# Long attention rows: a plain maximum for the unmasked half, taken as the initial value of the masked half's fused minimum

## The reference

```
att = q @ k.T * scale                      # (1024, 1024) for each of 2 x 16 heads
att = where(causal, att, -inf)
att = softmax(att, axis=-1)                # needs the maximum of each row's unmasked part
y   = att @ v
```

## Time and profile before

| what | value |
|---|---|
| median of three runs | 2633.96 us |
| lowest and highest run | 2629.57 and 2639.21 us |
| span of the profiled execution | 2632.3 us |
| TensorE, busy share of the span | 2535.4 us, 96% |
| VectorE | 1533.2 us, 58% |
| ScalarE, GpSimd | 1035.6 us (39%), 981.6 us (37%) |
| line 1501, 768 fused row pieces, busy | 413.2 us, mean 574 ns |

### The profile page before, as it was taken

How to read it: one execution, slowest core, us unless ns; L and a number is a source line. 1 busy time by engine, 2 the same in 40 slices (tenths; PEclk the granted TensorE clock), 3 DMA queues, 4 the chain that set the end, 5 groups by cost and what they waited for, 6 DMA issues and landing times.

```text
span 2632.3 us, 44135 instructions
## 1 busy us (share of the span) xinstructions
PE 2535.4 (96%) x16928; PEld 2013.0 (76%) x16928; DVE 1533.2 (58%) x3356; ACT 1035.6 (39%) x1885; POOL 981.6 (37%) x1373
## 2 busy tenths in 40 slices
PE   6999989999999999999999999999999999999999
PEld 4788867667668888888888878677776678888887
DVE  7777579979975445433333345798589643333333
ACT  6555346656653223311111133566466431111111
POOL 5333566666643225211111122666366521111110
PEclk9999989999999999999999999999999999999999
DMA  4222131222220110100000002343233100000001
GB/s 148 73 73 73 39 76 46 51 68 64 48 93 1 36 45 12 37 25 25 24 25 25 25 17 58 92 94 75 52 88 79 37 32 25 24 25 25 25 17 64
DMA packets 72002, 128.73 MB, mean 49 GB/s; under 512 B 15728, under 2 KB 24944, under 8 KB 71792
## 3 DMA queue, kind: packets, MB, share of 16 engines
q1 hardware_dynamic: 71792, 125.92, 17.3%
HBM read 62.42 MB, written 13.63 MB: 29 GB/s over the span
## 4 chain that ended last, share of the span: by engine, by line
PE 81%; DVE 6%; POOL 2%; ACT 2%; SPq 2%; issue 2%; DMA 1%; DVEq 0%; ACTq 0%; POOLq 0%
PE psum L1049 65%; PE psum L1167 5%; PE psum L1130 4%; PE psum L1148 4%; PE psum L1178 2%; DVE psum L1501 2%; SPq L1745 1%; PE psum L1058 1%; DVE s1a0rden L1540 1%; ACT s1a0e L1335 1%; SPq L1764 0%; POOL s1a0e L1671 0%; ACT s4a1e L1335 0%; PE psum L1137 0%; POOL rstd L1610 0%
## 5 line engine op out<-in xcount | busy, mean ns | idle before, releaser
L1501 DVE CUSTOM_DVE_ANT_0 psum<-psum,mask_q 128x512 f32<-128x512 f32 (+5 forms) x768 | 413.2, 574 | 101.2 <-PE psum L1130 97.3
L1049 PE MATMUL psum<-hA_hi,wmem 128*128 128x256 f32 (+1 forms) x1536 | 405.2, 334 | 0.5 <-DVE s1a0negmax L1501 0.3
L1049 PEld LDWEIGHTS psum<-hA_hi,wmem 128*128 128x128 f32 x1536 | 270.3, 190 | 31.8 <-DVE s1a0negmax L1501 1.5
L1049 PE MATMUL psum<-hA_lo,wmem 128*128 128x512 f32 (+1 forms) x864 | 293.8, 340 | 0.0
L1335 ACT ACTIVATE s4a1e<-psum,p_scale 128x384 f32<-128x384 f32 (+5 forms) x384 | 205.5, 581 | 95.2 <-PE psum L1148 91.8
L1335 ACT ACTIVATE s1a0e<-psum,p_scale 128x384 f32<-128x384 f32 (+5 forms) x384 | 202.4, 578 | 78.1 <-PE psum L1148 76.8
L1454 DVE SCALAR_TENSOR_TENSOR x<-psum,x 128x512 f32<-128x512 f32 x256 | 175.7, 689 | 97.4 <-PE psum L1049 93.9
L1425 DVE TENSOR_TENSOR s5f1prod<-psum,s5f1silu 128x512 f32<-128x512 f32 x64 | 44.2, 691 | 303.7 <-PE psum L1049 303.7
L1425 DVE TENSOR_TENSOR s3f1prod<-psum,s3f1silu 128x512 f32<-128x512 f32 x64 | 44.2, 691 | 294.2 <-PE psum L1049 294.2
L1635 POOL TENSOR_TENSOR wmem<-raw,wmem 128x512 fp32r<-128x512 f32 x58 | 74.3, 1290 | 315.7 <-ACT wmem L1237 315.7
L1049 PE MATMUL psum<-s3f1w,s3f1a 128*128 128x512 f32 x768 | 181.6, 390 | 0.9 <-POOL s3f1w L1635 0.9
(11 more groups left out here) (195 smaller groups left out, 5581.8 us busy)
## 6 DMA issues: line engine op xcount, KB each, us to landing
s1a0qst<-s1a0qs SPq DMA_DIRECT2D x96, 128.0 KB, 2.3
s4a1qst<-s4a1qs SPq DMA_DIRECT2D x96, 128.0 KB, 2.4
s4a1kst<-s4a1ks SPq DMA_DIRECT2D x96, 128.0 KB, 2.4
raw<-in_gate SPq DMA_DIRECT2D x44, 256.0 KB, 2.9
raw<-in_up SPq DMA_DIRECT2D x44, 256.0 KB, 2.8
raw<-in_down SPq DMA_DIRECT2D x44, 256.0 KB, 2.8
rounded<-s0f0w SPq DMA_DIRECT2D x24, 256.0 KB, 2.0
s2f0w<-rounded SPq DMA_DIRECT2D x24, 256.0 KB, 4.9
```

The costliest lines, as they stand in the source:

```text
L1049: ins = pe.matmul(out_, w, m, start=n == 0, stop=n == len(terms) - 1)
L1501: dve.tensor_tensor_reduce(scores, scores, mask_q[:, first:first + pw], -1.0, -MASKED, ALU.add, ALU.min, T[s]["negmax"][n % 2][:, column:c ...
```

## The change

In a tile of two pieces, piece 0 becomes a plain `tensor_reduce` (maximum, negated) that reads the scores in PSUM and writes only the column `i` of `negmax`. Piece 1 stays the fused operation, but takes its initial value from that column instead of the constant, and writes the same column. It now waits for piece 0's result. The step row_min is gone with its semaphore, `negmax` has 8 columns instead of 12, and what waited for row_min (m_tp, and the next stage's begin) waits for the head's last row piece. Tiles of one piece are as before. No other step is moved.

```diff
                 if i == ST - 1:
-                    plan.append(("row_min", s, n))
                     side.start(timed((M_AFTER[0], ("m_tp", s, n)), (M_AFTER[1], ("m_hi", s, n)),
...
-                    t["negmax"] = [sbuf(sc, f"{tag}negmax{i}", [P, ST + CT]) for i in range(2)]
+                    t["negmax"] = [sbuf(sc, f"{tag}negmax{i}", [P, ST]) for i in range(2)]
...
-                    (sem["row_min"], at("row_min", "row_min", p, HEADS_ALL - 1)),
+                    (sem["row_max"], at("row_max", *last_row(p, HEADS_ALL - 1))),
...
+        def last_row(s, n):
+            return "row", s, n, LAST_ROW, row_pieces(LAST_ROW) - 1
...
             def m_tp(s, n):
                 ps = bank_of(("m_tp", s, n))
-                on.wait_ge(sem["row_min"], at("row_min", "row_min", s, n))
-                pe.transpose(ps[0:ST, 0, 0:P], T[s]["negmax"][n % 2][:, 0:ST],
+                on.wait_ge(sem["row_max"], at("row_max", *last_row(s, n)))
+                pe.transpose(ps[0:ST, 0, 0:P], T[s]["negmax"][n % 2][:],
                              ident[:]).then_inc(sem["m_tp"], 1)
...
                 first = SEQ - width + z * pw
-                column = i + z * CT
-                dve.tensor_tensor_reduce(scores, scores, mask_q[:, first:first + pw], -1.0, -MASKED,
-                                         ALU.add, ALU.min,
-                                         T[s]["negmax"][n % 2][:, column:column + 1]
-                                         ).then_inc(sem["row_max"], 1)
-
-            def row_min(s, n):
-                negmax = T[s]["negmax"][n % 2]
-                on.wait_ge(sem["row_max"], at("row_max", "row", s, n, LAST_ROW,
-                                              row_pieces(LAST_ROW) - 1))
-                dve.tensor_tensor(negmax[:, ST - CT:ST], negmax[:, ST - CT:ST],
-                                  negmax[:, ST:ST + CT], ALU.min).then_inc(sem["row_min"], 1)
+                negmax = T[s]["negmax"][n % 2][:, i:i + 1]
+                if z + 1 < row_pieces(i):
+                    dve.tensor_reduce(negmax, scores, AX.X, ALU.max,
+                                      negate=True).then_inc(sem["row_max"], 1)
+                    return
+                if z:
+                    on.wait_ge(sem["row_max"], at("row_max", "row", s, n, i, z - 1))
+                dve.tensor_tensor_reduce(scores, scores, mask_q[:, first:first + pw], -1.0,
+                                         negmax if z else -MASKED, ALU.add, ALU.min,
+                                         negmax).then_inc(sem["row_max"], 1)
```

More of the change, by code:

```diff
@@ L424 @@
     "bias_x": ("x_pool",),
-    "row": ("s_q", "row_max"), "row_min": ("row_min",), "m_tp": ("m_tp",), "m_hi": ("m_hi",), "m_lo": ("m_lo",),
+    "row": ("s_q", "row_max"), "m_tp": ("m_tp",), "m_hi": ("m_hi",), "m_lo": ("m_lo",),
     "key": ("s_k", "exp"), "e_mask": ("e_mask",), "pv": ("pv",),
@@ L1572, in vector_program @@
                      "q8": q8_, "q_b": q_b, "gu": gu, "a_lo": a_lo, "down": down,
-                     "turned": turned, "row": row, "row_min": row_min, "m_lo": m_lo, "v_out": v_out,
+                     "turned": turned, "row": row, "m_lo": m_lo, "v_out": v_out,
                      "y_fin": y_fin, "y_lo": y_lo, "x_sum": x_sum, "piece_lo": piece_lo}
```

## The result

The changed kernel takes 2660.84 us at the median of four runs (2652.24 to 2663.47). The kernel before, run beside it on the same chip, takes 2636.59 us (2629.57 to 2640.09). The ratio is 1.0091, with a 95% interval of 1.0067 to 1.0114: **24 us slower**. The forecast was 2645 us with a range of 2624 to 2661, +11 us. The sign was right and the time lies 0.2 us inside the range, but the increase was more than twice the forecast, and above the +19 that I had called its upper end. Of the 16 us between 2645 and 2660.84, 2.6 are the kernel before itself, whose median is 2636.59 here and was 2633.96 in the three runs known at the forecast.

The account below looks back on a forecast made before the run. TensorE and VectorE were taken to bound the attention stages together. Pairs +51 us against row_min's 41.6 freed, exposed between +4 and +19, gave +11: 2632.3 + 11 = 2643.3, plus 1.7 for the median, 2645 us; range 2624 to 2661.

Parts of the forecast that it names:

- its upper end: Attention stages: all pairs count, +51 us, less 32 us freed by the 44 row_mins not followed by VectorE idle time: +19.
- The gap: Between pieces 0 and 1 on VectorE: waiting for the own engine's result delays piece 1 by 0.11 us, as in the division.
- the bound of 0.04: Between pieces 0 and 1: the cheap case of the gap, 0.04 us, from an instruction with one wait.
- the exposed time: Both attention stages: the share of VectorE's added and freed time reaching the end, between +4 and +19, middle +11 us.
- the pairs' +5.5 and +51: Long tiles' 256 pairs: exposed cost +5.5 us if only the present chain counts, +51 us if all pairs count.
- the row_mins' -1.5 and -32: Removed row_mins: -1.5 us for the one long one in the chain, or -32 us for the 44 without idle time behind.
- The present chain's 10.7%: Line 1501 in both attention stages: 44 of its 413 us busy lie in the chain of waits; used for the lower end.
- The cover holds: Rival: VectorE's idle time takes up what is not in the chain now; +4 us, 2638 us, chance 0.31.
- The long row_mins were what hurt: Rival: eight row_mins over 1.4 us all delay TensorE, so removing them is faster; -9.4, 2624.6 us, chance 0.08.
- The wait costs nothing: Rival: piece 0's result is ready in time, a pair costs only +0.03 us; about -12, 2622 us, chance 0.05.
- The pointer meets GpSimd: Rival: piece 1, with mask and column in SBUF, stalls as row_min does; half exposed +50, 2695 us, chance 0.05.
- the plain maximum has another speed: Rival: piece 0 at 417 ns, about -24, 2610 us, chance 0.02; or at the reciprocal's rate, near 3200 us, chance 0.02.

Follow-up runs that it names:

- experiments 2 to 4: Three kernels, each the kernel before with one part: piece 1's wait (+29 us), piece 1's initial value from SBUF (+9 us), piece 0 as plain maximum (-6 us).
- experiment 1: The kernel before without row_min, the transposition taking columns 0 to 7 as they are: ratio 0.9971, -7.6 us.
- experiment 7: The kernel before with row_min as a tensor_reduce over pairs of neighbouring columns, one SBUF input instead of two: ratio 0.9994, -1.6 us.
- experiment 2: The kernel before with only the wait added, piece 1 of a long tile waiting for piece 0's result: ratio 1.0110, +29 us.
- experiment 5: The changed kernel with piece 1 of a tile put behind piece 0 of the next tile: ratio 1.0014, +4 us against the kernel before.

## Why the prediction was right, and where it was mis-sized

**The parts on VectorE.** The plain maximum was forecast at the fused piece's 0.69 us and lasts 0.683. The fused piece with the pointer was forecast at 0.75 and lasts 0.759. The gap was taken as 0.11 from the division; it is 0.144, and the bound of 0.04 was the row of an operation with one wait. For the pair of 512 I had 1.50 us and it takes 1.51. But I worked the sum on one pair and multiplied it by 256. That pair stood right behind an accumulator read, where it took 1.30 us before; only 16 of the 64 pairs of 512 do. The other 48 took 1.26 before and take 1.50 now. At the medians the pairs pay +0.247 us at 320 and at 512 and +0.240 at 448. With 0.24 a pair it is 62 us, not 51.

**The step that failed is the exposed time**, "so I take the middle, +11 us". The middle was made of two middles: of the pairs' +5.5 and +51, which is +28, and of the row_mins' -1.5 and -32, which is -17. Measured, the pairs cost +29 + 9 - 6 = +32 us (experiments 2 to 4) and the row_mins gave back 7.6 (experiment 1). So 9 of the 13 us that were missing are credit for row_min that never came, and 4 are the pairs. One common factor for both places was the error. I had written that "the two do not lie in equal places", and then had weighed them alike. The rows gave a hint of the difference: the earlier trace rows had 20 of 64 row_mins with VectorE idle right behind them, and I used that only to trim the upper end. Idle time that comes a few instructions later takes up time just as well: in experiment 1 VectorE waited 34 us longer for the scores, and those 20 hold only 7.8. The stalls, 25 us of the credit and in the earlier trace rows in plain sight, were worth 1.6 us (experiment 7).

**What was luck.** That 2660.84 lies inside the range at all is luck in part. The range went up to 2661 to leave 8 us for a plain maximum 0.03 us slower than the fused piece. The maximum is not slower; the wrong credit for row_min and the longer pairs used up the room that was left for it.

**The other bound.** The present chain's 10.7% of the pairs' time was a lower end too far down: half of it was paid (32 of 62). In the second stage, where 28 of the 35 us of idle time ahead of the 512-key pieces stood, I expected the gap to vanish, and the stage grew by 11.0 us against the first's 12.6. Idle time until the scores took up 16 of the wait's 63 us (experiment 2), not most of it. In the changed kernel the two lines together wait longer for TensorE than line 1501 did (97.3 us), as it did in experiment 1 without row_min. Line 1509, then line 1504, us and times:

```profile
  PE psum L1132: 51.2, 39
...
  PE psum L1132: 60.0, 70
```

So VectorE has 51.2 + 60.0 = 111 us of such waits and the program is slower all the same: slack ahead of one piece doesn't pay for a gap inside another. That the scores in turn wait for a bank which a longer pair frees later would explain it; no run here takes that apart.

**A term that was missing** is TensorE's clock. The granted clock over the span, before and after:

```profile
core 0: 2632.3 us, clock 0.992
...
core 0: 2657.3 us, clock 0.990
```

With the two levels 2.4 and 1.2 GHz a mean of 0.990 means that 0.020 of the span ran at the lower one and that half of it, 26.6 us, was lost to a TensorE that had work; before it was 0.008 of 2632.3, 21 us. The profiled execution of the wait alone has 0.988, 32 us:

```profile
core 0: 2665.1 us, clock 0.988
```

The mean over the runs is 0.989 for the changed kernel and 0.991 for the kernel before (in the runs beside the experiments), so some 5 of the 24 us are seen there. A clock of 1.00 and 0.98 in two dense stretches told me that no such wait hid there, and I took from it that none would come. The stretches that I hadn't read had room for it: from 330 to 400 us the kernel before was granted 0.90. After the change 500 to 600 us has 0.95 where it had 0.98, and 1580 to 1700 us 0.94 where it had 0.97, but 330 to 400 us has 0.95. No run here separates the clock from the stalls: which of them came first isn't shown, and with three digits the 5 us are good to about 2.

**The rivals.** *The cover holds* (+4 us) is excluded by the interval and by kernel 2: the program paid about half of the pairs' time (32 of 62 us), not the ninth of the chain. *The long row_mins were what hurt* fell twice: taking the join out gave 7.6 us, and ending all its stalls (experiment 7) gave 1.6 with an interval that includes nothing. *The wait costs nothing* fell at once, with 0.144 us ahead of every piece 1 and +29 us for the wait alone. The Trainium skill's page "VectorE: DVE Perf Modes", section "The DRAIN you can't avoid", says that chained operations take the same time with a semaphore after each as without. That does not hold here for a row piece that waits for its direct predecessor's result; with another piece between the two, experiment 5 agrees (-0.04%, uncertain by some 0.3%). *The pointer meets GpSimd* and *the plain maximum has another speed* fell to 761 ns at the most and 683 ns.

So the forecast's sign came from the right mechanism, a dependence put between neighbours on an engine that paces its stage, and its number was half because it was set against a credit that for the most part never came.

## What to carry to other kernels

Before an operation is merged away, price what it frees and what its successor pays apart: here a microsecond of VectorE was worth 0.18 where the join was taken out (and 0.06 where only its stalls were) and 0.34 to 0.46 where a filler or the wait lengthened a pair, and one cheap side step for each head was replaced by four short stalls. A row piece that needed the result of the piece right ahead of it made the pair a quarter of a microsecond longer, and the program measurably slower; with one other piece between the two nothing could be measured. If a chain can't be avoided, put work in between (a second wait moved elsewhere may help too; not tried here), or keep independent results and join them later, here with a `tensor_reduce` over one SBUF input, which never stalled. And a fall in busy time says nothing where a gap took its place: read the order of time.

## What the runs showed that I had not expected

- The start of a fused piece behind a wait for the piece ahead of it comes 0.14 us after the end of what it waits for, whatever its width and with or without a pointer; the `tensor_tensor` of the division starts after 0.10 with two waits and after 0.03 with one. I had taken the 0.10 (read as 0.11) for the fused piece as well.
- A plain `tensor_reduce` over PSUM lasts 683 ns for 512 elements, no more than the fused operation's 706, and a pair with it is 51 ns shorter, since nothing has to read an accumulator. Alone it gained 6 us; beside it only the missing join gained, and that came with the wait.
- The stalls of a small operation, up to 2.1 us long and 14 us in the eight longest together, were worth about nothing where they lay.
- The runs of one kernel differ by over 10 us, and they follow the clock: the kernel before was granted 0.993 in a run of 2631.0 us and 0.988 in one of 2645.0, 14 us for 0.005, where 0.005 of the span is 13 us. So two single executions of one kernel can differ by half a per cent, more than most of the parts measured here, and only the ratios over several runs tell them apart.
